# In the fused stage's TensorE queue, transposes and gate products move ahead of the output projection

## The chip, the cores and the metric

One core of one Trainium2 chip runs the whole program. The metric is device time in microseconds (us) of one execution. The engines are TensorE (PE, with its weight loads PEld), VectorE (DVE), ScalarE (ACT), GpSimd (POOL) and SyncE (SP), each with a queue of its own that it works off in order, and they meet by semaphores.

## The reference, cut to what matters

A block of two layers over 4 x 2048 tokens of 512 values: linear attention with random features, then a mixture of 32 experts of which each token takes 4.

```python
qkv = layernorm(x) @ w_qkv.T                      # 16 heads of 32
q_phi, k_phi = exp(features(rope(q))), exp(features(rope(k)))
S, sum_k = einsum(k_phi, v), sum(k_phi)           # per sequence and head
heads = (q_phi @ S) / max(q_phi @ sum_k, 1e-6)    # numerator, denominator
x1 = x + layernorm(heads @ w_out.T)               # output projection
xn = layernorm(x1)
scores = sigmoid(xn @ gate_w.T)                   # 32 gates per token
idx = top_k(scores + bias, 4)                     # and a slot of that expert (512 slots each)
out = sum of the 4 chosen experts' outputs, weighted, + a shared expert
result = x1 + layernorm(out)
```

## The kernel before, in words

The program has four stages: projection to q, k, v; sums over the keys; the fused stage `attend_and_route_stage`; experts and combination. The change lies in the fused stage alone. It takes the 8192 tokens as 16 groups of 512 (index n), each of four tiles of 128 tokens (A = 4, NT = 64 tiles, index m) and, for attention, of four sets of four heads (index q). Every engine's queue is a loop over steps s (`STEPS` is 85) that is unrolled when the program is built, and in step s an engine works on several tiles of different age. The lags are a table of constants: `PROJECT, MEASURE, SCALE, ADD, SPLIT, TURN, COPY, GATE = 8, 9, 10, 11, 12, 13, 14, 14` and `SCORE, CHOOSE, PLACE, WEIGH, FILL, SEND = 18, 18, 19, 19, 21, 21`.

TensorE's step s before the change: logits of the first half of unit s+1 (`make_logits`, L875); numerators of s (`add_numer`, L885); logits of the second half (L875); denominators (`add_total`, L894); the output projection of tile s-8 (`project`, 12 matmuls, L906); the 8 transposes of tile s-13 (`turn`, L918); the 8 gate products of tile s-14 (`make_gates`, L932); and in one step of four the counts of chosen experts (`count`, L942 to L945).

There is one tile `logits` in PSUM for both halves. So the second half's logits wait until ScalarE has read the first half (`phi_ready`), and so on. There is one tile `turned` in PSUM as well, so the transposes of tile m wait until ScalarE has copied tile m-1 out of it (`xT_ready`), and the gate products of tile m-1 read what that copy wrote:

```python
def turn(m):
    pe.wait_ge(x_low_ready, m + 1)
    if m >= 1:
        pe.wait_ge(xT_ready, m)
def make_gates(m):
    pe.wait_ge(xT_ready, m + 1)
def project(m):
    if m >= 2:
        pe.wait_ge(z_ready, m - 1)
```

ScalarE's step s: `make_phi(s+1, 0)` (L976), `make_z(s-10)` (L997), `read_numer(s)` (L984), `make_phi(s+1, 1)` (L976), `copy_turned(s-14)` (L1019, the copy that `turn` and `make_gates` of the same step wait for), `normalize(s-12)` (L1005 and L1011), and in one step of four `make_at_high` (L990).

VectorE's step s: `make_shift(s-10)` (L1125), `make_low(s-13)` (L1156), `add` (L1137), `measure_y(s-9)` (L1130), `measure_x1`, `aggregate`; and, one kind in each of the four steps of a group: `read_total` at the start and `make_share` (L1106) at the end; `fill` (up to L1205); `divide` (L1111) and `choose` (L1161 to L1174); `make_at_low` and `weigh`. Below these steps are called the group's first, second, third and fourth. `make_share` waits for a round trip of the denominators through DRAM, `divide` for a second one. GpSimd's step: `make_rstd(s-9)`, which `make_shift` of the next step needs, then four indirect DMAs (`send`, L1271) that write the tile's slots; a group's first one waits for `fill`.

Of the kernel before, what the change touches and what calls it, by code (L numbers as in the profile page):

```python
# [757 lines left out]
def attend_and_route_stage(nc, io, keep):  # L758
# [5 lines left out]
    with ExitStack() as ctx:  # L764
        t = Tools(nc, ctx, "s4")
        PHIS, XS = 4, 3
        NT = A * NG
        Y_SCALE = AT_SCALE * W_SCALE
        PROJECT, MEASURE, SCALE, ADD, SPLIT, TURN, COPY, GATE = 8, 9, 10, 11, 12, 13, 14, 14
# [50 lines left out]
        def group_at(s, lag):  # L820

            return (s - lag) // A if s >= lag and (s - lag) % A == 0 and (s - lag) // A < NG else None
# [41 lines left out]
        def _(pe):  # L864
            def make_logits(q, b):
                n, c = q // EC, q % EC
                if c == 0 and b == 0:
                    if n == 0:
                        pe.wait_ge(keep["ahead_loaded"], 128)
                    else:  # L870
                        pe.wait_ge(q_loaded[n % 2], 64 * ((n + 1) // 2))
                if q + b >= 1:
                    pe.wait_ge(phi_ready, 2 * q + b)
                for h in range(2):
                    mm = nc.tensor.matmul(logits[:, 512 * h:512 * h + 512], keep["feat"][:, HPC * c + 2 * b + h, :],  # L875
                                          qT[n % 2][:, HPC * c + 2 * b + h, :], start=True, stop=True)
                mm.then_inc(logits_ready, 1)

            def add_numer(q):
                n, c = q // EC, q % EC  # L880
                pe.wait_ge(phi_ready, 2 * q + 2)
                if q >= 1:
                    pe.wait_ge(numer_read, q)
                for i in range(HPC):
                    mm = nc.tensor.matmul(numer[D * i:D * i + D, :], keep["sumv"][:, n // GPC, HPC * c + i, :],  # L885
                                          phi[(2 * q + i // 2) % PHIS][:, i % 2, :], start=True, stop=True)
                mm.then_inc(numer_ready, 1)

            def add_total(q):
                n, c = q // EC, q % EC  # L890
                if c == 0 and n >= 1:
                    pe.wait_ge(den_ready, n)
                for i in range(HPC):
                    mm = nc.tensor.matmul(total[D * i:D * i + D, :], keep["sumk"][:, n // GPC, HPC * c + i, :],  # L894
                                          phi[(2 * q + i // 2) % PHIS][:, i % 2, :], start=(c == 0), stop=(c == EC - 1))
                mm.then_inc(total_ready, 1)

            def project(m):
                n, a = m // A, m % A
                if a == 0:  # L900
                    pe.wait_ge(at_low_ready, n + 1)
                if m >= 2:
                    pe.wait_ge(z_ready, m - 1)
                for c in range(EC):
                    for i, (s, w) in enumerate(((0, 0), (0, 1), (1, 0))):
                        mm = nc.tensor.matmul(y[m % 2][:], at_hl[n % 2][:, s, c, a * P:(a + 1) * P],  # L906
                                              keep["wo"][:, w, c, :], start=(c == 0 and i == 0),
                                              stop=(c == EC - 1 and i == 2))
                mm.then_inc(y_ready, 1)

            def turn(m):
                n, a = m // A, m % A
# [3 lines that stand above are left out]
                for s in range(2):  # L916
                    for c in range(EC):
                        mm = nc.tensor.transpose(turned[:].bitcast(F16)[:, (s * EC + c) * P:(s * EC + c + 1) * P],  # L918
                                                 hl[n % 2][:, a, s, c * P:(c + 1) * P], keep["ident16"][:])
                mm.then_inc(turned_ready, 1)  # L920

            def make_gates(m):
                n, a = m // A, m % A
                pe.wait_ge(xT_ready, m + 1)
                if n >= 1:
                    if a == 0:
                        pe.wait_ge(score_ready, n)
                    if a == 2:
                        pe.wait_ge(where_ready, n)
                for c in range(EC):  # L930
                    for s in range(2):
                        mm = nc.tensor.matmul(gates[:, a * NE:(a + 1) * NE], xT[n % 2][:, s, c, a * P:(a + 1) * P],  # L932
                                              keep["gate"][:, c * NE:(c + 1) * NE],
                                              start=(c == 0 and s == 0), stop=(c == EC - 1 and s == 1))
                if a == A - 1:
                    mm.then_inc(gates_ready, 1)

            def count(n):
                pe.wait_ge(mask_ready, n + 2)
                for a in range(A):  # L940
                    out = position[:, a * NE:(a + 1) * NE]
                    nc.tensor.matmul(out, keep["tri"][:], mask[:, a, :], start=True, stop=False)  # L942
                    for b in range(a):
                        nc.tensor.matmul(out, keep["ones"][:], mask[:, b, :], start=False, stop=False)
                    mm = nc.tensor.matmul(out, keep["ones"][:], before_us[:], start=False, stop=True)  # L945
                mm.then_inc(position_ready, 1)
# [3 lines left out]
            for s in range(STEPS):  # L950
                if s + 1 < NT:
                    make_logits(s + 1, 0)
                if s < NT:
                    add_numer(s)
                if s + 1 < NT:
                    make_logits(s + 1, 1)
                if s < NT:
                    add_total(s)
                if 0 <= s - PROJECT < NT:
                    project(s - PROJECT)  # L960
                if 0 <= s - TURN < NT:
                    turn(s - TURN)
                if 0 <= s - GATE < NT:
                    make_gates(s - GATE)
                n = group_at(s, PLACE)
                if n is not None:
                    count(n)
# [800 lines left out]
```

## Time and profile before

| | us |
|---|---|
| three runs | 2147.43, 2157.99, 2160.95 |
| median | 2157.99 |
| the profiled execution, time | 2154.41 |
| the profiled execution, span from first to last instruction | 2152.6 |
| PE busy, share of the span | 1828.6 (85%) |
| DVE busy | 1205.9 (56%) |
| ACT busy | 1124.9 (52%) |
| POOL busy | 772.0 (36%) |

Times in the rows are counted from the first instruction of the span. A busy share says how long an engine had instructions in it, over all stages; it doesn't say which engine sets the end of a stage. For that, the waits in the stage are read.

### The profile page before, as it was taken

Reading aid. Unit: us, or ns where it says so; the run is one execution under the profiler, and the core shown is the slowest. Engines: PE = TensorE matmul, PEld = TensorE weight load, DVE = VectorE, ACT = ScalarE, POOL = GpSimd, SP = SyncE. Lnnn points to the kernel's source line nnn. Section 1 sums busy time; section 2 is a strip of 40 time slices with the busy share of each in tenths; the row PEclk is TensorE's granted clock in tenths of the full one; section 3 lists DMA queues with packets and bytes.
Section 4 is the critical chain, followed back from the end, with each engine's and each line's share of the span. In section 5 each row is a group of like instructions: output and inputs, shape, how many; then the busy total and the mean of one; then the engine's idle time right before and its main releaser. Section 6 shows DMA issues by size and latency. Waiting matters only on the chain. (4 is left out here: it accounts for less than half of the span.)

```text
span 2152.6 us, 33711 instructions
## 1 busy us (share of the span) xinstructions
PE 1828.6 (85%) x12976; PEld 890.7 (41%) x12976; DVE 1205.9 (56%) x2230; ACT 1124.9 (52%) x1371; POOL 772.0 (36%) x718
## 2 busy tenths in 40 slices
PE   8899999999979999799888898404999988987995
PEld 6444444444427877133333333202444444433342
DVE  7676667666650000158878888831444434435887
ACT  5564555545425665577777776402444444432443
POOL 0000000000000000025677788874777777751110
PEclk9999999999989999899999999756999999998998
DMA  7435353546238886578777875322789999876994
GB/s 257 144 123 187 108 200 106 163 148 211 90 113 220 212 211 160 131 182 238 217 213 221 249 219 169 137 72 90 168 194 267 250 257 227 176 138 169 352 343 155
DMA packets 187791, 403.05 MB, mean 187 GB/s; under 512 B 33780, under 2 KB 72052, under 8 KB 171008
## 3 DMA queue, kind: packets, MB, share of 16 engines
q1 hardware_dynamic: 83184, 222.41, 35.2%
q10 hardware_dynamic: 67584, 122.17, 16.3%
q0 software_dynamic: 36864, 56.32, 13.7%
q8 instruction: 103, 1.69, 0.3%
q14 instruction: 56, 0.46, 0.1%
HBM read 237.06 MB, written 174.98 MB: 191 GB/s over the span
## 5 line engine op out<-in xcount | busy, mean ns | idle before, releaser
L258 PE MATMUL s_proj<-s_xT,keep_wqkv 128*128 128x512 f16 x1536 | 341.8, 379 | 0.0
L1271 POOL DMA_INDIRECT slot_dram<-s_filled,s_slots x256 | 305.2, 1192 | 95.1 <-issue 72.9
L1415 POOL DMA_INDIRECT acc_dram<-s_y,s_slot x128 | 205.9, 1609 | 101.3 <-DMA acc_dram<-s_y,s_slot 47.1
L906 PE MATMUL s_y<-keep_wo,s_at_hl 128*128 128x512 f16 x768 | 194.7, 408 | 42.6 <-ACT s_z L997 42.6
L258 PEld LDWEIGHTS s_proj<-s_xT,keep_wqkv 128*128 128x128 f16 x1536 | 147.8, 98 | 183.2 <-issue 12.6
L237 PE MATMUL s_proj<-keep_wqkv,s_xT 128*128 128x512 f16 x768 | 179.7, 393 | 34.5 <-ACT s_xT L500 34.5
L1522 ACT ACTIVATE s_gate<-s_gates 128x512 f32<-128x512 f32 x96 | 57.3, 597 | 281.2 <-PE s_ups L1474 219.1
L339 POOL TENSOR_SCALAR s_rstd<-s_mv 128x4 f32<-128x4 f32 x16 | 16.0, 998 | 496.5 <-DVE s_mv L354 496.5
L518 ACT ACTIVATE s_hl<-s_rot 128x1024 f16<-128x1024 f32 x64 | 67.6, 1057 | 221.1 <-DVE s_rot L400 220.6
L1577 DVE SCALAR_TENSOR_TENSOR s_h<-s_gate,s_ups 128x512 f32<-128x512 f32 x96 | 65.9, 686 | 199.0 <-ACT s_gate L1522 199.0
L676 ACT ACTIVATE s_phi<-s_logits 128x1024 f32<-128x1024 f32 x128 | 131.1, 1024 | 84.5 <-PE s_logits L697 84.5
L387 DVE TENSOR_TENSOR s_by_cos<-s_proj,s_table 128x1024 f32<-128x1024 f32 x64 | 78.4, 1224 | 171.4 <-PE s_proj L258 171.4
L1513 ACT ACTIVATE s_xT<-s_turned 128x1024 f16<-128x1024 f16 x128 | 125.5, 1019 | 83.3 <-PE s_turned L1452 83.0
L976 ACT ACTIVATE s_phi<-s_logits 128x1024 f32<-128x1024 f32 x128 | 131.1, 1024 | 53.4 <-PE s_logits L875 52.7
L1452 PE MATMUL s_turned<-keep_ident,s_rows 128*128 128x128 f16 x1024 | 80.3, 223 | 84.5 <-DMA s_rows<-rows_dram,s_slot 76.2
L1404 POOL DMA_INDIRECT s_rows<-rows_dram,s_slot x128 | 132.2, 1033 | 47.1 <-issue 36.9
L906 PEld LDWEIGHTS s_y<-keep_wo,s_at_hl 128*128 128x128 f16 x768 | 74.0, 103 | 179.2 <-issue 57.0
L737 PE MATMUL s_parts<-s_phi,s_v 128*33 128x128 f32 x2048 | 138.6, 278 | 2.2 <-DMA s_v<-v_dram 2.1
L1474 PE MATMUL s_gates<-s_xT,s_w 128*128 128x512 f16 x512 | 124.4, 387 | 18.6 <-issue 9.7
L1488 PE MATMUL s_ys<-s_w,s_parts 128*128 128x512 bf16 x512 | 132.1, 382 | 3.5 <-DVE s_y L1592 3.5
L237 PEld LDWEIGHTS s_proj<-keep_wqkv,s_xT 128*128 128x128 f16 x768 | 75.3, 101 | 132.0 <-ACT s_xT L500 42.2
L1474 PE MATMUL s_ups<-s_xT,s_w 128*128 128x512 f16 x512 | 121.3, 380 | 0.0
(164 smaller groups left out, 3217.0 us busy)
## 6 DMA issues: line engine op xcount, KB each, us to landing
s_x<-x_in SPq DMA_DIRECT2D x32, 1024.0 KB, 9.8
qk_dram<-s_hl ACTq DMA_DIRECT2D x32, 1024.0 KB
keep_ahead<-qk_dram SPq DMA_DIRECT2D x48, 512.0 KB
acc_dram<-s_zero SPq DMA_DIRECT2D x17, 1024.0 KB, 11.5
v_dram<-s_v ACTq DMA_DIRECT2D x16, 1056.0 KB, 5.8
s_v<-v_dram SPq DMA_DIRECT2D x16, 1056.0 KB
s_spread<-share_dram SPq DMA_DIRECT2D x64, 256.0 KB, 4.6
x_dram<-s_x ACTq DMA_DIRECT2D x16, 1024.0 KB, 4.9
```

What stands on the lines that cost most here:

```text
L237: mm = nc.tensor.matmul(proj[half][:, 512 * b:512 * b + 512], left, right, start=(c == 0 and i == 0), stop=(c == EC - 1 and i == 2))
L258: mm = nc.tensor.matmul(out[:, 512 * b:512 * b + 512], left, right, start=(c == 0 and i == 0), stop=(c == EC - 1 and i == 2))
L676: nc.scalar.activation(phi[n % 2][:].rearrange("p h m -> p (h m)"), logits[n % 2][:], ACT.Exp, scale=1.0 / M_SCALE).then_inc(phi_ready, 1)
L737: mm = nc.tensor.matmul(parts[ch % 2][at:at + D + 1, h // 2 * M:(h // 2 + 1) * M], v[n % 2][:, a * H + h, :], phi[half][:, h % HALF, :], s ...
L906: mm = nc.tensor.matmul(y[m % 2][:], at_hl[n % 2][:, s, c, a * P:(a + 1) * P], keep["wo"][:, w, c, :], start=(c == 0 and i == 0), stop=(c ...
L976: nc.scalar.activation(phi[m % PHIS][:].rearrange("p h q -> p (h q)"), logits[:], ACT.Exp, scale=1.0 / M_SCALE).then_inc(phi_ready, 1)
L1271: nc.gpsimd.indirect_dma_start(out=io["slot"], out_offset=bass.IndirectOffsetOnAxis(ap=slots[n % 2][:, a * K + j:a * K + j + 1], axis=0), ...
L1404: nc.gpsimd.indirect_dma_start(out=rows[r][:, a, :], out_offset=None, in_=io["rows"], in_offset=bass.IndirectOffsetOnAxis(ap=slot[e % RING ...
L1415: nc.gpsimd.indirect_dma_start(out=io["acc"], out_offset=bass.IndirectOffsetOnAxis(ap=slot[e % RING][:, a, 0:1], axis=0), in_=y[e % 2][:, ...
L1474: mm = nc.tensor.matmul(bank[:], w[:, c, i * P:(i + 1) * P], left[:, s, c, :], start=(c == 0 and s == 0), stop=(c == EC - 1 and s == 1))
L1488: mm = nc.tensor.matmul(ys[a % 2][:], parts[e % 2][:, i, s, a * P:(a + 1) * P], w[:, i, :], start=(i == 0 and s == 0), stop=(i == IC - 1 a ...
L1513: nc.scalar.activation(xT[k][:, :, :, a * P:(a + 1) * P], turned[a % 2][:].bitcast(F16).rearrange("p (s c q) -> p s c q", s=2, c=EC), ACT. ...
```

## The change

In TensorE's step the call of `project` moves from ahead of `turn` and `make_gates` to behind them. Nothing else is edited: the same instructions and the same semaphores, and the queues of ACT, DVE, POOL and SP are as they were.

```diff
                 if s < NT:
                     add_total(s)
-                if 0 <= s - PROJECT < NT:
-                    project(s - PROJECT)
                 if 0 <= s - TURN < NT:
                     turn(s - TURN)
                 if 0 <= s - GATE < NT:
                     make_gates(s - GATE)
+                if 0 <= s - PROJECT < NT:
+                    project(s - PROJECT)
                 n = group_at(s, PLACE)
                 if n is not None:
                     count(n)
```

TensorE's queue in a whole step in the middle of the stage, before (the s_y row is the output projection, s_turned the transposes, the first s_route row the gate products, s_hl the split rows that are transposed):

```order
568 L875 MATMUL s_logits<-keep_ahead,keep_feat 128x512 x2
569 L885 MATMUL s_numer<-s_phi,keep_sumv 32x512 x4
570 L875 MATMUL s_logits<-keep_ahead,keep_feat 128x512 x2
571 L894 MATMUL s_total<-s_phi,keep_sumk 32x512 x4
572 L906 MATMUL s_y<-keep_wo,s_at_hl 128x512 x12
573 L918 MATMUL s_turned<-keep_ident,s_hl 128x128 x8
574 L932 MATMUL s_route<-keep_gate,s_xT 128x32 x8
575 L942 MATMUL s_route<-s_mask,keep_tri 128x32
```

The same place of the same queue in the changed kernel:

```order
568 L875 MATMUL s_logits<-keep_ahead,keep_feat 128x512 x2
569 L885 MATMUL s_numer<-s_phi,keep_sumv 32x512 x4
570 L875 MATMUL s_logits<-keep_ahead,keep_feat 128x512 x2
571 L894 MATMUL s_total<-s_phi,keep_sumk 32x512 x4
572 L918 MATMUL s_turned<-keep_ident,s_hl 128x128 x8
573 L932 MATMUL s_route<-keep_gate,s_xT 128x32 x8
574 L906 MATMUL s_y<-keep_wo,s_at_hl 128x512 x12
575 L942 MATMUL s_route<-s_mask,keep_tri 128x32
```

The 12 matmuls of the projection stood between the denominators and the transposes, and now stand behind the gate products; the counts keep their place at the step's end. At the end of the stage, where the logits have run out (the step after the last one that has them), TensorE's queue before:

```order
957 L932 MATMUL s_route<-keep_gate,s_xT 128x32 x8
958 L885 MATMUL s_numer<-s_phi,keep_sumv 32x512 x4
959 L894 MATMUL s_total<-s_phi,keep_sumk 32x512 x4
960 L906 MATMUL s_y<-keep_wo,s_at_hl 128x512 x12
961 L918 MATMUL s_turned<-keep_ident,s_hl 128x128 x8
962 L932 MATMUL s_route<-keep_gate,s_xT 128x32 x8
```

and in the changed kernel:

```order
957 L906 MATMUL s_y<-keep_wo,s_at_hl 128x512 x12
958 L885 MATMUL s_numer<-s_phi,keep_sumv 32x512 x4
959 L894 MATMUL s_total<-s_phi,keep_sumk 32x512 x4
960 L918 MATMUL s_turned<-keep_ident,s_hl 128x128 x8
961 L932 MATMUL s_route<-keep_gate,s_xT 128x32 x8
962 L906 MATMUL s_y<-keep_wo,s_at_hl 128x512 x12
```

Here too the projection follows the gate products. The copy that both `turn` and `make_gates` wait for is ScalarE's last but two in its step.

## Rows read from the trace of the kernel before

**Rows 1.** Timeline, PE, one step: start, us, engine, line, operation [idle before <-releaser]

```profile
1150.47 0.59 PE L875 MATMUL s_logits<-keep_ahead,keep_feat 98*128 98x512 f16 x2
...
1153.71 2.76 PE L906 MATMUL s_y<-keep_wo,s_at_hl 128*128 128x512 f16 x12
1156.31 0.61 PE L918 MATMUL s_turned<-keep_ident,s_hl 128*128 128x128 f16 x8
1156.76 0.35 PE L932 MATMUL s_route<-keep_gate,s_xT 128*128 128x32 bf16 x8
1156.96 0.59 PE L875 MATMUL s_logits<-keep_ahead,keep_feat 98*128 98x512 f16 x2
```

**Rows 2.** Timeline, ACT, the same step

```profile
1151.10 1.02 ACT L976 ACTIVATE s_phi<-s_logits 128x1024 f32<-128x1024 f32 x1 [0.96 <-PE s_logits L875]
1152.02 0.77 ACT L997 ACTIVATE s_z<-s_y,s_shift,s_rstd 128x512 f32<-128x512 f32 x1
...
1154.06 1.04 ACT L1019 ACTIVATE s_xT<-s_turned 128x1024 f16<-128x1024 f16 x1
```

**Rows 3.** Timeline, PE: the first logits of steps 14 and 62

```profile
942.58 0.60 PE L875 MATMUL s_logits<-s_qT,keep_feat 98*128 98x512 f16 x2
...
1310.63 0.59 PE L875 MATMUL s_logits<-s_qT,keep_feat 98*128 98x512 f16 x2
```

**Rows 4.** Timeline, PE: a group's fourth step ends with counts, the next step begins

```profile
1143.42 0.35 PE L932 MATMUL s_route<-keep_gate,s_xT 128*128 128x32 bf16 x8
...
1143.97 0.59 PE L875 MATMUL s_logits<-keep_ahead,keep_feat 98*128 98x512 f16 x2
```

**Rows 5.** Waits, 980 to 1280 us: who <- for whom: us, times, longest

```profile
PE s_y L906 <- ACT s_z L997: 17.2, 10, 5.0
```

**Rows 6.** Timeline, all engines: a group's third and fourth steps (from 1156.96 and 1163.49)

```profile
1158.55 0.69 DVE L1130 BATCH_NORM_STATS2 s_stats<-s_y 128x6 f32<-128x512 f32 x1
...
1160.70 2.29 DVE L1111 TENSOR_TENSOR s_heads<-s_heads,s_spread 128x2048 f32<-128x2048 f32 x1 [0.66 <-DMA s_spread<-share_dram]
...
1165.91 0.61 PE L875 MATMUL s_logits<-s_qT,keep_feat 98*128 98x512 f16 x2 [0.83 <-ACT s_phi L976]
...
1166.73 1.03 DVE L1174 TENSOR_REDUCE s_mask<-s_onehot 128x128 f16<-128x512 f32 x1
...
1168.70 2.76 PE L906 MATMUL s_y<-keep_wo,s_at_hl 128*128 128x512 f16 x12 [1.20 <-ACT s_z L997]
```

**Rows 7.** Timeline, DVE and POOL: three late events in the middle of the stage

```profile
1013.89 0.69 DVE L1099 TENSOR_SCALAR s_den<-s_total 128x512 f32<-128x512 f32 x1
...
1025.72 0.55 DVE L1106 RECIPROCAL s_share<-s_dens 128x64 f32<-128x64 f32 x1 [8.26 <-DMA s_dens<-den_dram]
...
1130.73 2.29 DVE L1111 TENSOR_TENSOR s_heads<-s_heads,s_spread 128x2048 f32<-128x2048 f32 x1 [3.88 <-DMA s_spread<-share_dram]
...
1226.36 1.25 POOL L1271 DMA_INDIRECT slot_dram<-s_filled,s_slots  x1 [6.58 <-issue]
```

**Rows 8.** Timeline, POOL: the stage's end

```profile
1311.62 1.50 POOL L1271 DMA_INDIRECT slot_dram<-s_filled,s_slots  x1 [0.20 <-issue]
...
1341.35 1.39 POOL L1271 DMA_INDIRECT slot_dram<-s_filled,s_slots  x1 [1.01 <-DVE s_slots L1205]
...
1460.17 0.97 POOL L1271 DMA_INDIRECT slot_dram<-s_filled,s_slots  x1 [0.30 <-issue]
```

**Rows 9.** Timeline, PE: projections and logits behind waits

```profile
1027.17 5.30 PE L906 MATMUL s_y<-keep_wo,s_at_hl 128*128 128x512 f16 x12 [4.97 <-ACT s_z L997]
...
1189.92 0.60 PE L875 MATMUL s_logits<-s_qT,keep_feat 98*128 98x512 f16 x2 [1.47 <-ACT s_phi L976]
1191.46 2.76 PE L906 MATMUL s_y<-keep_wo,s_at_hl 128*128 128x512 f16 x12
...
1289.72 0.61 PE L875 MATMUL s_logits<-s_qT,keep_feat 98*128 98x512 f16 x2 [0.97 <-ACT s_phi L976]
...
1292.52 4.29 PE L906 MATMUL s_y<-keep_wo,s_at_hl 128*128 128x512 f16 x12 [1.20 <-ACT s_z L997]
```

## The prediction

> **What bounds the kernel now.** The views were read in this order: the page's busy shares, the timeline of a plain step of the fused stage, the waits of its middle, and the timeline of each engine where a step is longer. The busy shares name TensorE (85%), but they are a mean over four stages; the change touches one, some 600 us long.
>
> In a plain step TensorE hardly waits [rows 1]: one set of logits starts at 1150.47, the next step's at 1156.96, so the step is 6.49 us, and no row in it names a wait of any length. ScalarE has slack in it: it idled 0.96 us before its first exponential [rows 2]. What the reader is to see is the order of the two queues. ScalarE's copy of the transposed tile is its fifth piece and ends at 1154.06 + 1.04 = 1155.10, 4.63 us after TensorE began the step. TensorE comes to the transposes, which wait for that copy, at 1156.31, 5.84 us after. The 2.60 us of projection in between (1153.71 to 1156.31) cover it with 1.2 us to spare.
>
> The steps are not all plain. From step 14, the first whose transposes need a copy, to step 62, the last with logits, TensorE took 1310.63 - 942.58 = 368.05 us for 48 steps [rows 3]. Eleven of them hold the counts; there 0.55 us lie between gate products and next logits [rows 4] where a plain step has 0.20 [rows 1], so 0.35 more each, 3.9 in all. 48 x 6.49 = 311.5. What is left, 368.1 - 311.5 - 3.9 = **52.7 us**, are stalls: on z ahead of the projection (17.2 us in 300 us, [rows 5]), on exponentials ahead of the logits, and matmuls at the lower clock level behind long stalls. Most belong to a group's fourth step. There VectorE is late: it divides at 1160.70, finishes choosing at 1166.73 + 1.03, and so the projection waited 1.20 us [rows 6].
>
> **The change, term by term.** No instruction is added or removed, and no queue but TensorE's is altered. Three things follow.
>
> (1) *The cover is gone.* TensorE is ready for the transposes at 1153.71, 3.24 us into the step. The copy ends at 4.63, plus 0.05 for the semaphore: a wait of 4.68 - 3.24 = **1.44 us**. Can the copy come earlier? ScalarE's first exponential needs the step's first logits, and the second one stands ahead of the copy and needs the second logits. The whole chain starts when TensorE starts the step, so ScalarE's slack doesn't help. Nor is the loss made up behind: gate products need the same copy, and the projection stands behind both. The step becomes 4.68 + 3.25 (projection, transposes, gate products: 1153.71 to 1156.96, [rows 1]) = 7.93 us. Over 48 steps that is 48 x 1.44 = **+69.1 us**.
>
> (2) *The old stalls.* A step that is 1.44 us longer gives VectorE and GpSimd time. Walked for a group with counts (4 x 7.93 + 0.35 = 32.07 us): the projection now ends at about the start of the next step (+0.16), and `measure_y` of that step waits for it. From its start to the division at 1160.70 with 0.66 us of DMA wait inside, VectorE took 2.15 - 0.66 = 1.5 us [rows 6], so in the third step it can divide at +1.7. From the division to the end of choosing it took 1167.76 - 1160.70 = 7.06, which lands at +8.8 of the third step, +0.8 of the fourth. ScalarE asks for the shift at +1.55 (z in [rows 2] began 1152.02 - 1150.47 = 1.55 into the step). So the wait on z is gone, and so is the one on the exponential, since the split of the heads now fits in ScalarE's longer idle time. In a normal group all the old stalls are hidden: **-52.7 us**.
>
> Part of them comes back, where the cause is a late DMA or GpSimd [rows 7]. The share of 1025.72 ended 12.4 us after its denominators were read at 1013.89; read at the start of the first step (-0.3), they would give a share at +12.1, 4.2 us into the second step, and z would be 2.6 us late. With the 1.44 this is a stall of 4 us, and behind one of 4.97 us the projection took 5.30 us instead of 2.76 [rows 9]: 2.6 + 2.5. The division that waited 3.88 us at 1130.73: 0.65 us are to spare (shift at +0.8, needed at +1.45), and the two longer steps between denominators and division absorb up to 2.9 more, so 0.3 to 3.2 us; I take 1.0, near the lower end, because the steps' starts don't depend on the DMA. GpSimd's pause of 6.58 us, less the 1.44 us a step that it gains in three or four steps: 0.8 to 2.3, I take 1.4. Sum 7.5. The bytes are the same and the time longer, so I take **+6 us**, between 0, if nothing of the sort falls badly, and +12, if it falls more often.
>
> (3) *The end of the stage.* Without logits GpSimd's indirect DMAs set the pace. From 1311.62 to the last at 1460.17 it waited once, for 1.01 us [rows 8]. It stays so; the projection comes some 1.7 us later in those steps (copy 1.0, transposes 0.45, gate products 0.20), but VectorE needs it only in the step after. GpSimd begins step 61's DMAs 1.0 us after the start of step 62 (1311.62 - 1310.63); in the changed kernel up to 3 us ahead of it, so at most 4 us are won. VectorE's pieces then decide up to 1341.35: the division comes at +1.7 instead of +3.7 (1160.70 - 1156.96), less some 0.8 for the later projection: **-1.2 us**, between -4 and, if the projection turns out to be waited for in every such step, +4.
>
> Sum: 69.1 - 52.7 + 6 - 1.2 = **+21 us**; I take **+20**, since the late events are drawn anew. The profiled execution took 2154.41 us (span 2152.6 and 1.8 around it) and would take 2174; the median of the runs shown is 3.6 us higher, so the forecast is 2157.99 + 20 = **2178 us**. Its own range, from the ends above: 16.4 + 0 - 4 = +12 to 16.4 + 12 + 4 = +32, 2170 to 2190.
>
> **A rule weighed against the rows.** The clock is the open price of the new stall, which is the same in every step. In the rows one stall of 1.47 us left the next projection at 2.76 us; a stall of 1.20 us, alone since the last logits, once left it at 2.76 [rows 6] and once at 4.29 [rows 9], the latter with another stall of 0.97 us ahead. So 1.44 us once in 7.93 is on the safe side, though not by much. The Trainium skill ("TensorE: Matmul & The Clock Gate", section "A second HAM failure mode: psum-queue depth-cycling") says that a TensorE that idles briefly but often between groups of matmuls sees its clock go back and forth between the levels, and loses throughput by it. By that rule the sum would be rival 1's; by the rows it stays at +20.
>
> **The rivals.**
>
> *Rival 1, the clock falls in plain steps.* For: the stall is regular, and the matmuls around it (numerators, denominators) are narrow. Against: [rows 9] as above. Price: a slow projection costs 4.29 - 2.76 = 1.5 to 5.30 - 2.76 = 2.5 us; one step in three, 16 x 2.0 = 32 on top of 20: about 2210 us.
>
> *Rival 2, the loss is mostly given back.* GpSimd's last 150 us start when the last groups' slots are ready, and late events don't recur: 69.1 - 52.7 - 4 = +12, and 2 less if the step's chain through ScalarE is 0.05 shorter than in the row: +10, 2168 us. For: GpSimd hardly waits from 1311.62 on. Against: the middle's floor, 32.07 us a group, doesn't depend on GpSimd.
>
> *Rival 3, faster.* The 52.7 us of old stalls go, and the new wait is shorter than I think, because the copy gets done earlier. It decides at 52.7 / 48 = 1.10 us a step: if the copy ended less than 4.3 us into the step, the change would gain. With a wait of 0.5 us: 24 - 52.7 = -29, 2129 us. Against: each piece ahead of the copy is pinned by TensorE's own logits [rows 2].
>
> *Rival 4, the order isn't what runs:* the listing of the changed program shows the projection behind the gate products in every step. No chance worth naming.
>
> **How the numbers follow.** Forecast 0.69, rival 1 0.12, rival 2 0.15, rival 3 0.04. About 1% (21.6 us) is what a measurement of this kernel can tell from no change, and the forecast lies at it: of its 0.69, 0.38 are below and 0.31 above. Faster by over 1%: 0.03. Within: 0.38 + 0.15 + 0.01 = 0.54. Slower: 0.31 + 0.12 = 0.43. The range that leaves no more than 0.2 out goes from 2166, just under rival 2, to 2199, between the forecast's own end and rival 1: outside lie most of rival 1, rival 3 and a few hundredths.
>
> **What the profile after would show.** TensorE waits before the transposes for ScalarE's copy (`PE s_turned <- ACT s_xT`), some 1.4 us a step and 60 to 75 us in the stage. Plain steps of 7.9 us, groups of 32.1 with few above 34. The wait of the projection on z nearly gone up to step 62, no wait of the fourth step's logits over 0.2 us. VectorE waits for the projection ahead of `measure_y`, at no cost. GpSimd waits more in the middle, for aggregates and slots. The prediction is wrong if plain steps aren't within 0.2 us of 7.93, if projections of plain steps take longer than 2.76 us, or if groups of the changed kernel show fourth steps over 8.5 us as a rule.

## The result, and the profile after

The changed kernel took **2205.16 us** (median of four runs, 2199.21 to 2218.19), the one before 2154.57 in the same comparison (four runs, 2147.43 to 2160.95). The ratio is 1.0219, 95% interval 1.0174 to 1.0265: slower by about 2.2%. Medians and ratios here and below leave out the runs in the chip's slower state, in which the same kernel takes over 1% longer. The forecast was 2178 with a range from 2166 to 2199, so the direction was right, the time lies outside the range, and more than half of the loss was missed. The profiled execution of the changed kernel took 2209.76 us, 55.4 more than the profiled one before (2154.41). The rest of this section says where these 55.4 us lie.

The page of the changed kernel begins:

```profile
span 2208.0 us, 33711 instructions
...
PE 1836.9 (83%) x12976; PEld 894.9 (41%) x12976; DVE 1209.8 (55%) x2230; ACT 1121.7 (51%) x1371; POOL 779.3 (35%) x718
```

The same instructions, and busy times that hardly differ from before; what grew is idle time. The timeline of TensorE in one plain step, which answers to [rows 1]:

```profile
1180.76 0.60 PE L875 MATMUL s_logits<-keep_ahead,keep_feat 98*128 98x512 f16 x2
...
1185.55 0.61 PE L918 MATMUL s_turned<-keep_ident,s_hl 128*128 128x128 f16 x8 [1.47 <-ACT s_xT L1019]
1185.99 0.36 PE L932 MATMUL s_route<-keep_gate,s_xT 128*128 128x32 bf16 x8
1186.19 2.75 PE L906 MATMUL s_y<-keep_wo,s_at_hl 128*128 128x512 f16 x12
1188.78 0.60 PE L875 MATMUL s_logits<-keep_ahead,keep_feat 98*128 98x512 f16 x2
```

and of ScalarE in the same step, which answers to [rows 2]:

```profile
1181.39 1.02 ACT L976 ACTIVATE s_phi<-s_logits 128x1024 f32<-128x1024 f32 x1 [2.57 <-issue]
...
1184.36 1.04 ACT L1019 ACTIVATE s_xT<-s_turned 128x1024 f16<-128x1024 f16 x1
```

The step is 1188.78 - 1180.76 = 8.02 us long. The transposes begin 0.15 us after the end of ScalarE's copy (1184.36 + 1.04 = 1185.40), and in front of them stands a wait of 1.47 us. The profile puts such a wait down to ScalarE's copy in 47 of the 48 steps, 72.1 us in sum, the longest 4.1. The waits between 980 and 1280 us, beside [rows 5]:

```profile
POOL s_rstd L1262 <- DVE s_mv L1150: 51.0, 20, 7.1
...
PE s_turned L918 <- ACT s_xT L1019: 52.6, 34, 4.1
...
DVE s_stats L1130 <- PE s_y L906: 17.0, 12, 3.5
```

The projection's wait for z, 17.2 us before, is in the list no more. GpSimd waits for aggregates, VectorE for the projection. The first logits of steps 14 and 62, which answer to [rows 3]:

```profile
944.04 0.60 PE L875 MATMUL s_logits<-s_qT,keep_feat 98*128 98x512 f16 x2
...
1363.13 0.60 PE L875 MATMUL s_logits<-s_qT,keep_feat 98*128 98x512 f16 x2
```

The stretch took 419.09 us where it took 368.05: **+51.0** of the 55.4. The last of GpSimd's slot sends, which answers to the last of [rows 8]:

```profile
1510.51 0.97 POOL L1271 DMA_INDIRECT slot_dram<-s_filled,s_slots  x1 [0.31 <-issue]
```

lies 147.4 us behind step 62, before it was 149.5: -2.2. Ahead of step 14 there are 1.5 us more, and in the stages behind, which the change doesn't touch, 5.1.

Of the 419.09, the step of 8.02 explains 48 x 8.02 + 11 x 0.35 (counts) = 388.8. There remain **30.3 us** of surplus: 20.7 in the first steps of groups, 7.4 in second steps (one alone has 4.9), 2.2 in fourth steps, none in third ones. The fourth steps, the sore point of before, are fine but for two (of 8.95 and 9.96 us). The first steps are new. The timeline of all engines where one begins (the L945 row is the last of the counts, which stand directly behind the projection):

```profile
1171.23 0.97 POOL L1271 DMA_INDIRECT slot_dram<-s_filled,s_slots  x1 [0.30 <-issue]
...
1171.36 0.18 PE L945 MATMUL s_route<-s_before_us,keep_ones 128*128 128x32 f16 x1
...
1171.39 0.59 PE L875 MATMUL s_logits<-keep_ahead,keep_feat 98*128 98x512 f16 x2
...
1172.66 0.29 DVE L1187 COPY s_where<-s_route 128x128 f32<-128x128 f32 x1 [1.20 <-PE s_route L945]
...
1173.38 1.02 ACT L976 ACTIVATE s_phi<-s_logits 128x1024 f32<-128x1024 f32 x1 [4.36 <-PE s_logits L875]
...
1174.46 0.61 PE L875 MATMUL s_logits<-keep_ahead,keep_feat 98*128 98x512 f16 x2 [1.48 <-issue]
```

By TensorE's own rows nothing is late: the counts take 0.025 us each and the logits follow at 1171.39. But those who wait for them say otherwise. VectorE reads the counts 1.1 us after their last row's end, and ScalarE begins the exponential 1.99 us after the logits' start, where in a plain step it is 0.63 (1181.39 - 1180.76). I call this distance the **lag**. It is 0.63 in all twelve first steps of before, and 1.2 to 2.1 in the ten first steps of after from step 24 on. In steps 16 and 20 it is 0.63 in after as well; GpSimd's sends begin only in step 21. The semaphores agree with the waiters: TensorE's signal that the counts ahead of 1171.39 are done came 1.10 us after their last row's end. In before such signals came 0.01 to 0.03 us after it (one of ten can't be matched). Behind such a lag there stand two waits in one step, and some of the matmuls then run at the lower level of the clock. Six projections of first steps did, for 7.3 us more in sum; this is the one of step 24:

```profile
1033.80 3.88 PE L906 MATMUL s_y<-keep_wo,s_at_hl 128*128 128x512 f16 x12
```

Three more were slow: one behind a wait of 4.1 us in step 25, and two, of 3.96 and 3.99 us, in steps 21 and 31, where the lag is 0.63 and the only long wait is the usual one of 1.47 us. So the clock did fall twice in steps that have nothing but the regular wait; each of the two is 1.6 us longer for it.

### The profile page after: what moved, and what is told of

It is laid out like the page before. It is cut to its first block and busy times, and to the rows that moved or that the text cites. A ratio compares the mean times of both kernels' runs of the same rounds, so it can differ in the third digit from the quotient of the medians.

```text
span 2208.0 us, 33711 instructions
## 1 busy us (share of the span) xinstructions
PE 1836.9 (83%) x12976; PEld 894.9 (41%) x12976; DVE 1209.8 (55%) x2230; ACT 1121.7 (51%) x1371; POOL 779.3 (35%) x718
## 5 line engine op out<-in xcount | busy, mean ns | idle before, releaser
L1271 POOL DMA_INDIRECT slot_dram<-s_filled,s_slots x256 | 290.3, 1134 | 107.3 <-issue 71.2
L258 PEld LDWEIGHTS s_proj<-s_xT,keep_wqkv 128*128 128x128 f16 x1536 | 147.8, 98 | 183.2 <-issue 12.6
L1513 ACT ACTIVATE s_xT<-s_turned 128x1024 f16<-128x1024 f16 x128 | 125.0, 1018 | 73.4 <-issue 61.0
L1474 PE MATMUL s_gates<-s_xT,s_w 128*128 128x512 f16 x512 | 128.4, 396 | 25.5 <-ACT s_xT L1513 14.5
L918 PE MATMUL s_turned<-keep_ident,s_hl 128*128 128x128 f16 x512 | 45.3, 240 | 117.0 <-ACT s_xT L1019 96.8
```

The lines of the kernel that those rows point to most:

```text
L258: mm = nc.tensor.matmul(out[:, 512 * b:512 * b + 512], left, right, start=(c == 0 and i == 0), stop=(c == EC - 1 and i == 2))
L1271: nc.gpsimd.indirect_dma_start(out=io["slot"], out_offset=bass.IndirectOffsetOnAxis(ap=slots[n % 2][:, a * K + j:a * K + j + 1], axis=0), ...
L1474: mm = nc.tensor.matmul(bank[:], w[:, c, i * P:(i + 1) * P], left[:, s, c, :], start=(c == 0 and s == 0), stop=(c == EC - 1 and s == 1))
L1513: nc.scalar.activation(xT[k][:, :, :, a * P:(a + 1) * P], turned[a % 2][:].bitcast(F16).rearrange("p (s c q) -> p s c q", s=2, c=EC), ACT. ...
```

## The experiments

Two questions were open: is the plain step's wait what the forecast said it was (ScalarE's copy too late), and where do the late first steps come from. "The stretch" is from step 14's first logits to step 62's, as above. Before has 368.05 in it, after 419.09.

**Counts ahead of the projection.** After, with the counts between gate products and projection.

```diff
-                if 0 <= s - PROJECT < NT:
-                    project(s - PROJECT)
                 n = group_at(s, PLACE)
                 if n is not None:
                     count(n)
+                if 0 <= s - PROJECT < NT:
+                    project(s - PROJECT)
```

> The changed kernel with the counts moved ahead of the projection too, so that TensorE's step ends with the projection. Of the changed kernel's 419 us between steps 14 and 62, 48 x 8.02 + 11 x 0.35 = 389 are the new plain steps; 21 of the other 30 lie in a group's first step, right behind the counts. Theory A (small matmuls right behind the projection start the next step late): the lag from the first logits to the first exponential in first steps falls from 1.2 to 2.1 us back to 0.63 us, and the low-clock projections behind it go too: about 20 us faster than the changed kernel, 2185 us. Rival B (late DMAs and the clock are drawn anew, the place of the counts is nothing): first steps as long as before, 9 to 12 us, time 2205 us as the changed kernel.

Measured: 2193.79 us, ratio to before 1.0151 (1.0107 to 1.0194). The stretch took 407.7. Theory A holds for most of the first steps, but the time is 9 us above the 2185 that it named. Nine of the twelve first steps are 8.02 us, three 9.6; the lag is 0.63 in eleven of them. The wait for the copy is unchanged (70.8 us). The first steps give back 16 us (117.0 to 101.0 in sum); the second ones take 4. So most of the first steps' surplus (16 of 20.7) hangs on the counts' place behind the projection, and it goes while the wait for the copy stays. The run doesn't say why the place is bad.

**The counts twice.** After, with the ten small matmuls issued two times over, to see whether the hidden cost grows with them.

```diff
-            def count(n):
+            def count(n, again=False):
...
+                if not again:
+                    count(n, True)
+                    return
                 mm.then_inc(position_ready, 1)
```

> The changed kernel with the 10 count matmuls issued twice in a row (the second pass writes the same values again). Theory A (the small matmuls behind the projection cost more than their rows show): the lag from the first logits to the first exponential of first steps grows by another 1 us or so beyond the 0.35 us of the added rows, first steps get 1.4 to 2 us longer, 16 to 25 us in all. Rival B (their place is nothing): +0.35 us a group, 5 us in all.

Measured: 2243.54 us, ratio 1.0391 (1.0365 to 1.0417). Theory A, and by more than it said: the first steps took 28 us more in sum. The fourth steps grew by the 0.35 us that the rows give, to 8.72, but the first steps to 12.6 to 13.2, with a lag of 3.3 to 4.2 from step 24 on. In steps 16 and 20 they stayed at 8.02 with 0.63. The timeline of this kernel at one of them:

```profile
1213.84 0.59 PE L875 MATMUL s_logits<-s_qT,keep_feat 98*128 98x512 f16 x2
...
1217.89 0.29 DVE L1190 COPY s_where<-s_route 128x128 f32<-128x128 f32 x1 [4.18 <-remote]
1217.93 1.02 ACT L979 ACTIVATE s_phi<-s_logits 128x1024 f32<-128x1024 f32 x1 [6.81 <-remote]
```

Ten more matmuls of 32 columns, each with a weight load of its own, raised the mean lag of these ten steps from 1.7 to 3.9 us: some 0.2 each, beside the 0.035 in the rows. It is a price of each matmul that TensorE's rows don't show and that is not there before the sends begin.

**The turn in front alone.** Transposes, projection, gate products, counts: one half of the change, and the gate products between projection and counts.

```diff
                 if 0 <= s - TURN < NT:
                     turn(s - TURN)
-                if 0 <= s - GATE < NT:
-                    make_gates(s - GATE)
                 if 0 <= s - PROJECT < NT:
                     project(s - PROJECT)
+                if 0 <= s - GATE < NT:
+                    make_gates(s - GATE)
```

> One part alone: TensorE's step makes the transposes first, then the projection, then the gate products, then the counts. ScalarE's order is that of after. Theory A (the step is lengthened by the transposes' place alone, since the gate products wait for nothing that is late): the transposes wait about 1.47 us for ScalarE's copy as in after, plain steps 8.0 us, 47 such waits, about 70 us. Rival B (the gate products in front of the projection also have a part in the plain step): plain steps under 7.9 us. On the groups' first steps: if the counts cost time only where they stand directly behind the projection, they come out at 8.0 to 8.4 us with 0.63 us from the first logits to ScalarE's first exponential, and the stretch from step 14 to step 62 takes about 400 us (after 419); the kernel's time is then some 2185 to 2195 us. If it is the projection's new place late in the step that counts, and not the neighbour, the first steps stay at 9 to 10 us and the time at 2200 us or more.

Measured: 2226.65 us, ratio 1.0286 (1.0223 to 1.0349), the stretch 435.21. Plain steps are 8.02 with 1.4 us of wait: theory A holds for those, and the gate products have no part in them. What I expected of the first steps was wrong. They are 10.5 to 12.9 us with a lag of 2.3 to 4.1. "Directly behind the projection" is not the condition, then. More small matmuls in a row at that place (8 and 10) cost more. In before the same 18 stand in a row at the step's end and have no lag; the reason is below, under the sends held.

**No sends.** After, with GpSimd's slot sends and the waits for them, VectorE's too, left out; the slot table isn't written, so the time is not that of the whole work.

```diff
-                if 0 <= s - SEND < NT:
-                    send(s - SEND)
-            for k in range(2):
-                pool.wait_ge(scattered[k], 16 * A * K * NG // 2)
```

> After with GpSimd's sends of the slots left out (the slot table isn't written, and VectorE's wait for those transfers is gone). It tells whether the counts behind the projection are late only beside those transfers, as the first group, whose counts come before the first send, had no delay. Theory A (the delay is TensorE's own, from small matmuls behind a long row of projection matmuls): first steps stay at 9 to 10 us, lag from first logits to first exponential 1.2 us or more, steps 14 to 62 about 410 to 419 us. Rival B (the sends' traffic delays the operands or the semaphores of the counts): first steps at 8.0 us and lag 0.63 us in every group, steps 14 to 62 about 390 to 398 us. The transposes' wait for ScalarE's copy stays at 1.47 us under both.

Measured: 2114.72 us, the stretch 388.85, to be held against 388.8 for steps of 8.02. All 48 lags are 0.63. Theory A (TensorE's own delay) fell, rival B holds, and more strongly than expected: *all* of the 30 us of surplus go with the sends, the slow projections too. The busy times of this kernel from 983 to 1298 us (the columns: length, then busy time and instructions of PE, PEld, DVE, ACT, POOL, then PE's granted clock, the DMA share, GB/s):

```profile
983.00:1298.00 315.00, 252.94 (x2007) 95.95 (x2010) 255.09 (x645) 224.94 (x292) 75.36 (x78) 1.00 0.73 216
```

and the same stretch of after:

```profile
983.00:1298.00 315.00, 245.85 (x1833) 92.86 (x1830) 234.31 (x587) 206.33 (x267) 205.45 (x202) 0.95 0.75 197
```

The clock is 1.00, though TensorE idles 1.47 us in every step. The sends' issue on GpSimd and their packets are both gone here, so this run doesn't tell the two apart.

**Before without sends.** The same edit on the kernel before, for the price of the order alone (again without the slot table).

> The kernel before with GpSimd's sends of the slots left out (the slot table isn't written). Beside after without sends (steps 14 to 62 in 388.9 us, 2114.7 us) it gives the price of the order alone. Theory A (the stalls of 52.7 us of before, that the forecast saw covered by the slower step, all come from the sends that keep GpSimd from its rstd; the order costs the full 1.5 us in each of 48 steps): steps 14 to 62 take 315 to 322 us, plain steps 6.49, TensorE's wait for ScalarE's z is gone, and the time is 2035 to 2055 us, some 73 below after without sends. Rival B (the old stalls have another source, such as the chain of VectorE's late transfers): the stretch stays at 340 to 368 us and the time at 2065 us or more.

Measured: 2071.32 us, the stretch 340.95. Theory A was too simple: 340.95 - 315.4 (48 x 6.49 + 3.9) = 25.5 us of stalls are left that have nothing to do with the sends. They stand where the forecast saw them. A fourth step of this kernel:

```profile
1145.10 0.59 PE L875 MATMUL s_logits<-s_qT,keep_feat 98*128 98x512 f16 x2
...
1147.37 0.60 PE L875 MATMUL s_logits<-s_qT,keep_feat 98*128 98x512 f16 x2 [0.68 <-ACT s_phi L976]
...
1149.31 2.76 PE L906 MATMUL s_y<-keep_wo,s_at_hl 128*128 128x512 f16 x12 [0.34 <-ACT s_z L997]
...
1156.17 1.07 PE L894 MATMUL s_total<-s_phi,keep_sumk 128*32 128x512 f32 x8 [0.94 <-DVE s_den L1099]
```

With the sends before's stalls are 52.7, so 27.1 come with the sends. Without sends the order costs 388.85 - 340.95 = **47.9 us**, with them 51.0.

**GpSimd busy, but no transfer.** After, with each send replaced by one power on GpSimd (no slot table).

```diff
-                    nc.gpsimd.indirect_dma_start(
-                        out=io["slot"],
...
-                        oob_is_err=False).then_inc(scattered[n % 2], 16)
+                    i = ((n % 2 * A + a) * K + j) * 3
+                    nc.gpsimd.tensor_tensor(spent[:, i:i + 3], one[:], half[:], ALU.pow).then_inc(scattered[n % 2], 16)
```

> After with each of GpSimd's 16 sends of a group replaced by one power of a 128x3 tile on GpSimd, of about 1 us (the slot table isn't written). GpSimd is then as busy at the same places, with no transfer issued. Theory A (what delays the counts behind the projection is the issue of the transfers or the transfers themselves): first steps 8.0 us with lag 0.63, steps 14 to 62 in 389 to 395 us. Rival B (any work of GpSimd at that time delays them, by its use of the memory or by its hold on VectorE): lag 1.2 to 2.1 in the first steps from step 24 on, first steps 9 to 10 us, stretch over 400 us.

Measured: 2126.79 us (one run), the stretch 388.80, all lags 0.63. A first step in the timeline of all engines:

```profile
1152.74 3.55 POOL L1275 TENSOR_TENSOR s_spent<-s_one,s_half 128x3 f32<-128x3 f32 x4
...
1154.50 0.59 PE L876 MATMUL s_logits<-keep_ahead,keep_feat 98*128 98x512 f16 x2
1154.69 0.29 DVE L1188 COPY s_where<-s_route 128x128 f32<-128x128 f32 x1
1155.13 1.02 ACT L977 ACTIVATE s_phi<-s_logits 128x1024 f32<-128x1024 f32 x1 [2.99 <-PE s_logits L876]
```

GpSimd works across the counts in all ten groups from step 23 on, and they are on time. What delays them is something that the sends do, not a busy GpSimd as such.

**Sends held.** After with all its work and one wait more: GpSimd holds the sends of a group's third and fourth tile until the next group's counts are in.

```diff
+                if a == 2 and n + 1 < NG:
+                    pool.wait_ge(position_ready, n + 2)
```

> After with one wait more: GpSimd holds the sends of a group's third tile until the counts of the next group are in, so that no send is under way while TensorE makes the counts; all the work is done. Theory A (the counts are late where they meet a send): first steps 8.0 us but for single ones with low clock, lag 0.63, steps 14 to 62 in 392 to 402 us (after 419), time 2180 to 2192 us. Rival B (the lag in the first steps is not tied to the time of the sends, but to the kernel's order): first steps 9 to 10 us, time at 2200 us or more.

Measured: 2190.89 us, ratio 1.0164 (1.0129 to 1.0199), the stretch 400.25. Theory A, within all its bounds. All twelve first steps are 8.02 with a lag of 0.63. One of them, all engines:

```profile
1163.53 0.18 PE L945 MATMUL s_route<-s_before_us,keep_ones 128*128 128x32 f16 x1
...
1163.55 0.59 PE L875 MATMUL s_logits<-keep_ahead,keep_feat 98*128 98x512 f16 x2
...
1163.74 0.29 DVE L1187 COPY s_where<-s_route 128x128 f32<-128x128 f32 x1
...
1164.18 1.02 ACT L976 ACTIVATE s_phi<-s_logits 128x1024 f32<-128x1024 f32 x1 [3.00 <-PE s_logits L875]
...
1164.49 1.04 POOL L1273 DMA_INDIRECT slot_dram<-s_filled,s_slots  x1 [2.49 <-PE s_route L945]
```

The order on TensorE is word for word that of after; only the time of the sends moved. The lag is made by sends that are issued while the small matmuls run. In the second steps 7.5 us of surplus are left, in the fourth ones 4.1.

Why does before, with its counts at the step's end too, have no lag? Its trace at one of them:

```profile
1170.37 2.26 DVE L1115 TENSOR_TENSOR s_at_hl<-s_heads,s_at_hl 128x2048 f16<-128x2048 f32 x1
...
1170.86 2.62 POOL L1271 DMA_INDIRECT slot_dram<-s_filled,s_slots  x1 [0.30 <-issue]
...
1172.28 0.18 PE L945 MATMUL s_route<-s_before_us,keep_ones 128*128 128x32 f16 x1
...
1172.31 0.59 PE L875 MATMUL s_logits<-s_qT,keep_feat 98*128 98x512 f16 x2
...
1172.94 1.02 ACT L976 ACTIVATE s_phi<-s_logits 128x1024 f32<-128x1024 f32 x1 [0.61 <-PE s_logits L875]
```

A send lies across the counts here as well, but it takes 2.62 us beside VectorE's subtraction of 2.26 us, where one of after takes 0.97. It is so in six of before's ten groups with sends; in the other four no send lies across the counts, or for 0.15 us at most. So before isn't free of sends at that time: it has them at a moment at which they are drawn out, and then the counts are on time. In after all ten counts have a send row of 0.97 to 1.04 us across them, for 0.2 to 0.5 us of the counts' 0.5. Nor is the old order safe: in the old order with the early copy (below) one group's counts meet a send of 0.97 us for 0.36 us, and their signal is 0.96 us late. Nor is a drawn-out send always harmless: with the early copy, in either order, the counts of step 23 meet one of 1.9 us and are 1.2 or 1.3 us late.

**The copy late.** After, with ScalarE's copy behind both pieces of its normalisation: a second dose of the wait.

```diff
-                if 0 <= s - COPY < NT:
-                    copy_turned(s - COPY)
                 if 0 <= s - SPLIT < NT:
                     normalize(s - SPLIT)
+                if 0 <= s - COPY < NT:
+                    copy_turned(s - COPY)
```

> After with ScalarE's copy of the turned rows behind both pieces of its normalisation instead of ahead of them. It doses the wait on which the prediction rests. Theory A (the plain step is the loop from the transposes through ScalarE's copy back to the next transposes, so each us of ScalarE's work put ahead of the copy lengthens the step by itself): the two pieces take some 1.6 to 1.7 us, so the wait grows from 1.47 to about 3.1 us and the plain step from 8.0 to about 9.6 us, 48 steps, some 75 us more: about 2280 us. Rival B (the step is bound by something else that the wait only fills): the step stays below 8.5 us and the time below 2225 us.

Measured: 2338.53 us, ratio 1.0793 (1.071 to 1.0877), 58 above what theory A said. One step on TensorE:

```profile
1279.90 0.59 PE L875 MATMUL s_logits<-s_qT,keep_feat 98*128 98x512 f16 x2
...
1286.12 0.91 PE L918 MATMUL s_turned<-keep_ident,s_hl 128*128 128x128 f16 x8 [2.92 <-ACT s_xT L1019]
...
1287.09 4.02 PE L906 MATMUL s_y<-keep_wo,s_at_hl 128*128 128x512 f16 x12
1290.94 0.60 PE L875 MATMUL s_logits<-s_qT,keep_feat 98*128 98x512 f16 x2
```

The wait grew to 2.9 us, close to the 3.1 of theory A: the step is the loop through ScalarE's copy. But the step is 11.04 us, not 9.6: transposes and projection run partly at the lower clock level. In 47 of 48 steps the projection took 3.5 to 5.2 us (4.02 here) instead of 2.75, for 73 us in sum. The forecast's first rival does happen, only not at this dose. Another reading: the lag in the first steps is 0.63 here. In the longer step GpSimd is through with its sends before the counts come (none was under way from 1 us ahead of the first logits to 4 us behind them).

**The copy early.** After, with ScalarE's copy directly behind its first exponential. Before's order with the same edit ran beside it.

```diff
+                if 0 <= s - COPY < NT:
+                    copy_turned(s - COPY)
                 if 0 <= s - SCALE < NT:
                     make_z(s - SCALE)
...
-                if 0 <= s - COPY < NT:
-                    copy_turned(s - COPY)
```

> The changed kernel with one edit in ScalarE's queue: the copy of the transposed tile comes directly behind the first exponential, ahead of z, the numerators and the second exponential. Theory A (the loss is the wait of the transposes for the copy, 1.47 us in each step): the copy then ends 2.6 us into the step, TensorE asks for it at 3.24, the wait is gone and plain steps are back to 6.5 us; z is no longer awaited by the projection, so some 20 to 50 us less than the kernel before: 2110 to 2135 us. Rival B (GpSimd or the DMAs set a floor near 31 us a group): plain steps 6.5 us but fourth steps longer, time as the kernel before, 2155 us. Rival C (transposes ahead of the projection cost in themselves): still over 2190 us.

> The kernel before (projection ahead of transposes) with the same edit in ScalarE's queue alone. Theory A: the transposes didn't wait for the copy here, so nothing is won; z comes 0.9 us later in each step and ends at 3.3 us, just when the projection asks for it, so the projection's waits on z grow in the steps where the shift is late: 0 to 15 us slower than before, 2155 to 2170 us. Rival (an early copy is good in itself, in any order): faster than before by as much as the other kernel with the early copy.

Measured: with after's order **2150.54 us**, ratio to before 0.9966 (0.9952 to 0.998), the stretch 363.93; with before's order 2157.42, ratio 0.9991 (0.9971 to 1.001), the stretch 364.34. In the first of the two, ScalarE and TensorE in a plain step:

```profile
961.64 1.02 ACT L976 ACTIVATE s_phi<-s_logits 128x1024 f32<-128x1024 f32 x1 [1.13 <-PE s_logits L875]
962.56 1.02 ACT L1019 ACTIVATE s_xT<-s_turned 128x1024 f16<-128x1024 f16 x1
```

```profile
961.01 0.60 PE L875 MATMUL s_logits<-keep_ahead,keep_feat 98*128 98x512 f16 x2
...
964.25 0.62 PE L918 MATMUL s_turned<-keep_ident,s_hl 128*128 128x128 f16 x8
...
967.50 0.60 PE L875 MATMUL s_logits<-keep_ahead,keep_feat 98*128 98x512 f16 x2
```

The copy ends 2.57 us into the step (962.56 + 1.02 - 961.01), ahead of TensorE's 3.24, the wait is gone and the step back at 6.49. That part of theory A holds; its time (2110 to 2135) was missed, and rival B named the time and the long fourth steps. Of the 363.93 us, 363.93 - 315.4 = 48.5 are stalls (315.4 = 48 x 6.49 + 3.9), nearly the 52.7 of before: with the step short again they are back. Rival C fell, and so did the rival of the run beside it. So the new order has no price that shows once the copy is early. This version beats both kernels, before by a third of a per cent, which is little but outside its measurement's uncertainty.

**Copy early, counts ahead.** Both remedies in one kernel.

> Both remedies together: TensorE makes transposes, gate products, counts and then the projection, and ScalarE copies the turned rows directly behind its first exponential. Theory A (the wait for the copy and the late counts are two separate costs, and both have a remedy): plain steps 6.5 us, first steps no longer than in the version with the early copy alone, time at or below that one's 2150.5 us, down to about 2143. Rival B (with the step at 6.5 us the counts ahead of the projection wait for VectorE's mask, which is late there): a wait of TensorE for the mask in the first steps, and a time of 2152 to 2165 us.

Measured: 2162.15 us, ratio 0.9997 (0.9968 to 1.0025), the stretch 368.82. Neither theory. The time lies where B put it, but no wait of TensorE for the mask is in the trace. Three of the fourth steps are 11.5 to 12.3 us long, and what makes them so isn't settled; in two of them the counts' signal is on time. It may be that there is no quiet place left to move the counts to: a step's four sends take some 5.1 us, of steps that are 6.5 us long here.

## Why the prediction came out as it did

*Term 1, the cover is gone: right, and 4 us too small.* The wait was put at 1.44 us and is 1.47, the step at 7.93 and is 8.02, 48 x (8.02 - 6.49) = 73.4 us instead of 69.1. The copy was seen to end 4.63 us into the step; it ended at 4.64 (1185.40 - 1180.76), but the transposes began 0.15 after it and not 0.05. Both doses (copy early, copy late) moved the step as the mechanism says.

*Term 2, the old stalls: half right, and here the forecast failed.* "In a normal group all the old stalls are hidden: -52.7", and 6 back. Measured: 30.3 us of surplus are left, so the term is -22.4 instead of -46.7, 24 us too good. The runs without sends split it. Of the 52.7 us, 25.5 are stalls of the chain through VectorE; the longer step hid these to the last, as walked (388.85 against 388.8). The other 27.1 come with GpSimd's sends. The forecast took them for a matter of waiting that a longer step cures. In after there are 30.3 us of surplus again: 18.8 where sends meet the counts (gone with the sends held), the rest in a late share (4.9, for which the forecast had 2.6 + 2.5), in two fourth steps and in low clock. Two steps of the reasoning failed. One is "In a normal group all the old stalls are hidden: -52.7": its walk followed VectorE and ScalarE, and put the sends at nothing where they run beside TensorE's counts. The other is "Eleven of them hold the counts; [...] so 0.35 more each", taken over unchanged into the groups of 32.07 us: the counts' price was read at their old time, where a send lies across them only when it is drawn out beside VectorE, and not asked for again at the new time, 1.5 us later in the step. There the counts cost 0.6 to 1.5 us more than their rows say, and with the low clock behind it first steps are 9.0 to 12.1 us instead of 8.02.

*Term 3, the stage's end: right.* -1.2 expected, -2.2 measured, and GpSimd's sends set its pace as before. The remaining 6.6 us of the 55.4 lie ahead of step 14 and in the stages behind the fused one, in one execution each; no run here separates them from chance. So 21.2 + 4.3 + 24.3 - 1.0 + 6.6 = 55.4.

*The rivals.* Rival 1 (the clock falls in plain steps) gave nearly the right number, 2210, for the wrong reason: of the 48 projections 39 stayed at 2.75 us, six of the nine longer ones stand in first steps with a lag and one behind a wait of 4.1 us, and the granted clock is 1.00 where the sends are left out. Its mechanism did show in two steps (21 and 31), at 1.6 us each, 3 us and not 32. The Trainium skill's rule ("TensorE: Matmul & The Clock Gate", section "A second HAM failure mode: psum-queue depth-cycling") is hardly borne out at a regular wait of 1.47 us: 2 of 48 steps with the sends, none without. In the run with the wait of some 2.9 us it is, with 47 of 48 projections slow. Rival 3 put the point of decision in the right place, the copy's end, but not its price. With the copy's end at 2.57 us the order does no harm: 2150.54 us with it and 2157.42 without, with intervals that overlap. But the 52.7 us of old stalls that rival 3 counted as won stay, with 48.5 left: what hid them was the longer step, not the order.

*The signs that were named.* The wait of 60 to 75 us for the copy, the vanished wait for z, GpSimd's waits and VectorE's were all seen. "Groups of 32.1 with few above 34" was not: of the nine whole groups from step 24 on, all took over 33.4 us and seven over 34. I had asked for fourth steps over 8.5 us and not for first steps. Nor did all projections keep to 2.76 us in steps without a lag, as the two above show.

**What is open.** Why a send delays small matmuls. Leaving out the sends removes both GpSimd's issue of the transfers and the transfers, and neither was tried alone. The traces point to the issue. In the version with the counts ahead, seven groups' counts have no send row across them, but 6 to 18 of the sends' packets (of 8 to 64 bytes) in the 0.5 us of their rows, and all seven are on time; the one whose counts a send of 1.04 us crosses is 2.36 us late. In after four groups' counts (steps 39, 47, 51 and 59) have a send row across them and no such packet in that time, and are 0.3 to 1.3 us late. Why a send that is drawn out beside VectorE mostly does no harm isn't known either; nor whether it is the 32 columns or the weight loads, one for each matmul, that make the small ones suffer. The gate products, eight of the same width, can suffer too: where a send crosses them in first steps, the projection behind them ended 0.8 us late (steps 28 and 36), and the next step has a lag of 1.05 or 1.07. The Trainium skill ("SBUF — State Buffer", section "SBUF: two separate sides") says that transfers and engines reach the memory by separate ports and that TensorE never waits on anyone there. If that is so, the delay isn't in the memory's ports; no run here shows where it is.

## What to carry to other kernels

When an engine's order is changed, the piece to look at first is the one on the *other* engine that the moved instruction waits for: here one line moved in ScalarE's queue decides between +2.2% and -0.3%. A longer step hides old stalls, and a step that is made short again brings them back. A cost read from a row holds for its place and time; ask again what runs beside the piece at the new time. And where the waiting engines start later than the producer's rows say, trust the waiters.

## What the hardware showed that was not expected

GpSimd's indirect sends delay groups of matmuls of 32 columns that run while they are issued: by about 0.1 us a matmul for ten (a mean lag of 1.7 us for 0.63), 0.2 for each of ten more (3.9 us), with nothing of it in TensorE's own rows; powers on GpSimd over the same counts delay nothing, and neither did the six sends of 2.6 us beside VectorE's subtraction in before. And of the clock: a wait of 1.47 us once in 8.02 left the granted clock at 1.00 without the sends, one of some 2.9 us once in 11 brought it to 0.81, as the busy times of the kernel with the late copy show over the same 315 us:

```profile
983.00:1298.00 315.00, 231.68 (x1437) 87.06 (x1436) 185.73 (x469) 163.75 (x209) 154.03 (x154) 0.81 0.56 155
```
